# A language-model tower layer: the inner maximum turned one step later, x turned by a DMA, attend products alternating

## The reference

```
h   = layernorm(concat(emb[x], window_mean(pca[x]) @ projw + projb) @ fusw + fusb) * ln_g + ln_b
X   = layernorm(h)
Q, V= per-head RMS norm of X @ Wq.T, X @ Wv.T      (16 heads of 16)
out = Q[l] . cumsum over l of (K outer V)          (K = X by heads)
h   = h + out
xn  = layernorm(h)
a   = quantised to 8 bits by its row's maximum(xn) @ ternary(w1).T
s   = silu(depthwise conv over 3 tokens(a))        (1024 inner channels)
h   = h + quantised to 8 bits by its row's maximum(s) @ ternary(w2).T
```

## Time and profile before

| what | value |
|---|---|
| median of 3 runs (lowest, highest) | 326.43 us (324.97, 331.29) |
| the profiled execution's own time | 326.3 us |
| its span, first to last instruction | 324.6 us |
| mean granted TensorE clock | 0.782 |
| busy PE, DVE, ACT, POOL | 244.4, 244.1, 155.6, 86.4 us (75%, 75%, 48%, 27%) |

### The profile page before, as it was taken

The page is one execution under the profiler, slowest core; times in us unless marked ns, Lnnn a source line. Parts: engine busy times, 40 slices in busy tenths (PEclk is TensorE's granted clock), DMA queues, the critical chain, the costliest instruction groups (busy, mean ns, idle before and its releaser), DMA issues.

```text
span 324.6 us, 4726 instructions
## 1 busy us (share of the span) xinstructions
PE 244.4 (75%) x1538; PEld 179.5 (55%) x1538; DVE 244.1 (75%) x667; ACT 155.6 (48%) x312; POOL 86.4 (27%) x122
## 2 busy tenths in 40 slices
PE   2547597699589975997599849986899589628534
PEld 0206466568366754785477637665667467515322
DVE  0976636765997799769976998599858996886671
ACT  1054114537563765366445752595248633635811
POOL 5020013024503440235023412251233313412300
PEclk9955789669957996699559965997589857975575
DMA  7381110110011002100210012000300030001000
GB/s 186 71 290 28 49 26 0 33 42 0 1 42 32 3 0 72 37 1 0 65 43 2 1 32 73 3 0 18 90 0 2 0 96 4 1 0 34 0 32 32
DMA packets 16745, 11.71 MB, mean 36 GB/s; under 512 B 2832, under 2 KB 15953, under 8 KB 16721
## 3 DMA queue, kind: packets, MB, share of 16 engines
q1 hardware_dynamic: 15248, 10.64, 11.7%
q10 hardware_dynamic: 1472, 0.77, 1.0%
HBM read 4.07 MB, written 2.10 MB: 19 GB/s over the span
## 4 chain that ended last, share of the span: by engine, by line
PE 42%; DVE 39%; issue 6%; POOL 5%; ACT 3%; DMA 1%; SPq 1%; POOLq 0%; DVEq 0%; ACTq 0%
PE PS L614 10%; PE PH L671 9%; DVE mx L971 8%; PE PA L565 5%; PE PO L628 5%; PE PO L645 4%; DVE xq L950 3%; DVE h L983 3%; POOL h L362 3%; DVE hid L961 3%; PE PY L685 2%; DVE y L1006 2%; DVE h L829 2%; DVE amax L935 2%; DVE xn L930 2%
## 5 line engine op out<-in xcount | busy, mean ns | idle before, releaser
L479 ACT ACTIVATE hid<-PH,cb_s,cw_x 128x256 f32<-128x256 f32 x64 | 36.1, 564 | 81.8 <-PE PH L671 81.6
L671 PE MATMUL PH<-xsT,w1q 128*128 128x256 f16 x256 | 50.6, 351 | 6.2 <-DVE hid L961 5.8
L375 POOL TENSOR_TENSOR hid<-hid,tap 128x508 f32<-128x508 f32 x32 | 40.7, 1271 | 44.1 <-DVE hid L961 44.1
L905 DVE TENSOR_TENSOR ST<-PS,tri 128x512 f32<-128x512 f32 x32 | 22.1, 690 | 29.1 <-PE PO L645 20.6
L614 PE MATMUL PS<-QP,KM 128*128 128x256 f32 x128 | 42.3, 465 | 0.0
L671 PEld LDWEIGHTS PH<-xsT,w1q 128*128 128x128 f16 x256 | 29.1, 125 | 19.3 <-DVE hid L961 10.6
L961 DVE SCALAR_TENSOR_TENSOR hid<-PH,cw_x,hid 128x254 f32<-128x254 f32 x64 | 29.7, 475 | 7.9 <-ACT tap L482 7.9
L645 PEld LDWEIGHTS PO<-VD,ST 128*64 128x64 f32 x512 | 30.4, 137 | 7.3 <-issue 6.1
L645 PE MATMUL PO<-VD,ST 128*64 128x32 f32 x512 | 33.0, 222 | 0.4 <-DVE ST L905 0.4
L614 PEld LDWEIGHTS PS<-QP,KM 128*128 128x128 f32 x128 | 26.9, 232 | 10.6 <-issue 7.1
L971 DVE TENSOR_REDUCE mx<-sl 128x256 f32<-128x1024 f32 x16 | 30.7, 1916 | 2.6 <-ACT sl L489 2.6
(11 more groups left out here) (138 smaller groups left out, 454.7 us busy)
## 6 DMA issues: line engine op xcount, KB each, us to landing
QP<-QT SPq DMA_DIRECT2D x32, 64.0 KB, 2.0
VD<-Vn SPq DMA_DIRECT2D x32, 64.0 KB, 2.0
out_dram<-y SPq DMA_DIRECT2D x8, 256.0 KB, 2.1
w_s<-in_w1T_dram SPq DMA_DIRECT2D x1, 1024.0 KB, 5.2
w_s<-in_w2T_dram SPq DMA_DIRECT2D x1, 1024.0 KB, 7.6
fusw_s<-in_fusw_dram ACTq DMA_DIRECT2D x1, 512.0 KB, 4.3
feat_p<-feat SPq DMA_DIRECT2D x7, 64.0 KB, 2.0
ids_b<-in_ids_dram SPq DMA_DIRECT2D x4, 64.0 KB, 4.2
```

Of the source, the lines that this page charges most:

```text
L375: nc.gpsimd.tensor_tensor(part, part, tap[:, c % 2, :, :, 0:T - 1], ALU.add).then_inc(tap0_ok, 1)
L479: nc.scalar.activation(hid[:, j, :, :].rearrange("p u t -> p (u t)"), hidps(j), ACT.Identity, bias=cb_s[:, j:j + 1], scale=cw_x[:, j, 1:2])
L671: ins = nc.tensor.matmul(hidps(j), w1q[:, k, j * 128:(j + 1) * 128], xsT_v[:, h, :, k, :], start=(n == 0), stop=(n == 2 * KC - 1))
L905: nc.vector.tensor_tensor(ST[k][:, :].rearrange("p (n l) -> p n l", l=C), PS[k][:, :].rearrange("p (n l) -> p n l", l=C), tri[:, None, :]. ...
```

## The change

Three edits. On PE `turn_max` of a pair moves from the end of its stage-c step to the next step, behind `scores(b, 0, 0)` and directly ahead of `spread_scale`; on DVE `hid_scales` moves from the end of the step to the next, behind `mask_state` and ahead of `quantise(d, 0)`. `transpose_xs` and `take_xs` go, with the f16 identity; SP issues one transposing DMA from xs to xsT, ahead of `spread_q`, and both `hidden` and the next `xs_high` wait for its completion. In `attend` the loops over chunk b and r are exchanged, and the state product comes first.

```diff
@@ sync @@
+            def turn_xs(g):
+                wait(sp, h_ps, 8 * g)
+                wait(sp, xs_ok, 2 * g + 2)
+                sp.dma_start_transpose(xsT[:, :].rearrange("p (n t) -> p n t", t=T),
+                                       xs[:, :, :, :].rearrange("p h u d -> p (h u d)")).then_inc(xst_ok, 16)
...
                 on(gather_features, first(a))
+                on(turn_xs, b)
                 on(spread_q, a)
                 on(store, d)
@@ scalar @@
-            act.wait_ge(pool_c, 9)
-            nc.scalar.activation(ident16[:, :], ident[:, :], ACT.Copy).then_inc(ident16_ok, 1)
...
             def xs_high(g, u):
                 wait(act, xq_ok, 2 * g + u + 1)
-                wait(act, xst_ps, g)
+                wait(act, xst_ok, 16 * g)
...
-            def take_xs(g):
-                wait(act, xst_ps, g + 1)
-                wait(act, h_ps, 8 * g)
-                nc.scalar.activation(xsT[:, :], HB[1][:, :].bitcast(F16), ACT.Copy).then_inc(xst_ok, 1)
...
-                on(take_xs, b)
@@ tensor @@
-                for b in range(2):
-                    if b == 1:
-                        nc.tensor.matmul(PO[C:T, to:to + 128], QT[:, k, u, C:T], BD[:, u * KC + k, :],
-                                         start=True, stop=False, skip_group_check=True)
-                    for r in range(NG):
-                        hp = NG * k + r
+                nc.tensor.matmul(PO[C:T, to:to + 128], QT[:, k, u, C:T], BD[:, u * KC + k, :],
+                                 start=True, stop=False, skip_group_check=True)
+                for r in range(NG):
+                    hp = NG * k + r
+                    for b in range(2):
...
-            def transpose_xs(g):
-                wait(pe, xs_ok, 2 * g + 2)
-                wait(pe, conv_ok, 8 * g)
...
             def hidden(g, j):
...
                 if j == 0:
-                    wait(pe, xst_ok, g + 1)
+                    wait(pe, xst_ok, 16 * g + 16)
...
                 on(scores, b, 0, 0)
+                on(turn_max, d)
                 on(spread_scale, d)
...
                 on(down, d)
-                on(transpose_xs, b)
                 on(sum_q, a)
-                on(turn_max, c)
@@ vector @@
                 on(mask_state, b)
+                on(hid_scales, d)
                 on(quantise, d, 0)
...
                 on(inv_roots_q, a, 3)
-                on(hid_scales, c)
```

More of the change, by code:

```diff
@@ L83, in lm_tower_kernel @@
         ident = sb("ident", [128, 128])
-        ident16 = sb("ident16", [128, 128], F16)
         ones = sb("ones", [128, 128])
@@ L183, in lm_tower_kernel @@
         pf_ps, pf_ok, tab_ps, tab_ok = sem("pf_ps"), sem("pf_ok"), sem("tab_ps"), sem("tab_ok")
-        ld_pf, ident16_ok = sem("ld_pf"), sem("ident16_ok")
+        ld_pf = sem("ld_pf")
         wabs_ok, wsum_ps, w_ok = sem("wabs_ok"), sem("wsum_ps"), sem("w_ok")
@@ L204, in lm_tower_kernel @@
         a_c = sem("a_c")
-        xq_ok, xs_hi, xs_ok, xst_ps, xst_ok = (sem(n) for n in ("xq_ok", "xs_hi", "xs_ok", "xst_ps", "xst_ok"))
+        xq_ok, xs_hi, xs_ok, xst_ok = (sem(n) for n in ("xq_ok", "xs_hi", "xs_ok", "xst_ok"))
         h_ps, tap1_ok, tap0_ok, conv_ok, silu_ok = (sem(n) for n in (
```

## The result

The changed kernel takes 343.1 us (median of 4 runs, 339.38 to 345.56) against 325.7 for the kernel before: a ratio of 1.052, with an interval of 1.041 to 1.063. Slower, and within a tenth of a microsecond of the 343.0 on record. Some executions of a kernel are 1.5% to 3% longer than its fastest, most of them at a lower granted clock; the medians of this document count them, the ratios and intervals leave them out.

A forecast was written before the change was run, and what follows sets the result against it. VectorE from the third mask to finish, then TensorE, was taken to bound each step; waits +13.8 and +2.5, front -4.5, DMA +0.9 and +1.8, attend -2.4, clock +4.6 gave +16.7 on 326.3: 343.0 us, range 328 to 362.

The forecast's parts named there:

- The path and its two halves: In a 34.3 us step VectorE bounds from the third mask to finish, then turn_max and TensorE's chain.
- The wait ahead of spread_scale: TensorE's spread_scale waits for the masks and hid_scales on VectorE: +2.3 us in each of steps 3 to 8, 13.8 us.
- The turning DMA: The DMA on SP that turns xs into xsT takes 4.5 us, between bounds of 2.1 and 16.
- The terms of +1.8 and +0.9 for steps 2 and 3: Hidden products start later, waiting for the DMA's xsT: +1.8 us in step 2, +0.9 in step 3.
- Step 9: hid_scales stands behind convs 0 and 1 on VectorE, so hidden product 2 starts 2.5 us later.
- Attend: Faster products in the attend call before the third mask: 0.3 us a call, eight pairs, -2.4 us.
- The clock: TensorE's clock rises later, after the second scores, in four of six steps: +4.6 us.
- rival 1: The DMA turning x is slow, making xsT last at the front of steps 2 to 9; 371 at 8 us; chance 0.20.
- Rival 2: Stall mostly repaid: DMA takes 2.1 us, clock doesn't mind, attend gains 0.5; +5.0, 331.3 us; chance 0.18.
- Rival 3: Without the pause before turn_max, TensorE's clock rises before state: 318.0 us; chance 0.12.
- front of steps 4 to 8: With turn_max gone from between sum_q and the hidden products, state starts 0.9 us earlier: -4.5 over five steps.

The follow-up runs named there:

- filler: Changed kernel with eight more f16 products, results unused, between turn_max and spread_scale on TensorE: 331.44 us, ratio 1.015.
- move_alone: Kernel before with only turn_max and hid_scales moved into the next step; x still turned on TensorE, old attend order: 352.13 us, ratio 1.086.
- scales_first: Changed kernel with hid_scales ahead of the two masks, mask_scores and mask_state, on VectorE: 341.96 us, ratio 1.050.
- dma_alone: Kernel before with only x turned by the DMA; turn_max and hid_scales at the end of their step, old attend order: 327.2 us, ratio 1.007.

## Why the prediction was right, and where it only came out right

- **The path and its two halves**: right. Vn took turn_max's place at the front. The rows of y in the chain of waits, in step 6 before and after:

```profile
193.60 0.79 DVE y L1006 x2
```

```profile
201.03 0.78 DVE y L989 x2
```

From y's start to state's start it takes 196.90 - 193.60 = 3.3 us before and 203.34 - 201.03 = 2.3 after: a gain of 1.0, the bound named, for the 0.9 put. VectorE's half, from the third mask to y, takes 19.2 us in steps 3 to 7 of both kernels (19.3 in step 6), so nothing was lost or won there.
- **The wait ahead of spread_scale**: the mechanism and place as put, with hscale as releaser. The term of +2.3 a step was mis-sized: 3.53 - 0.85 = 2.7. hid_scales took 208.66 to 209.68, 1.0, as put; what I missed is that spread_scale behind a pause adds its full 1.22 to the path, while behind running products its 1.06 from start to end overlaps the scores and adds 0.85. Its idle time was 1.89, put at 1.6.
- **The turning DMA**: 4.5 put, 3.1 measured, which is nearer to the store of the earlier trace rows. The terms of +1.8 and +0.9 for steps 2 and 3 are wrong by all of their size: step 2's third mask came 0.3 earlier than before, and step 3's first hidden product at 93.23, not 95.0. The Trainium skill's page "Advanced Engine Details and Errata" (X-Bar Transpose) has transposing DMAs as fast as others; the trace agrees only roughly, with 3.1 us for 256 KB against the 2.1 of the store. Its page "VectorE: DVE Perf Modes" (The three transpose paths) gives 1309 ns for one block of 128x128; no run here turns one block alone, and the estimate of 10.5 us that I worked out from it, for eight in a row, does not hold for one DMA with all eight.
- **Step 9**: +2.5 put at hidden product 2. From step 8's third mask it came 313.77 - 289.96 = 23.8 after, 296.24 - 274.62 = 21.6 before: +2.2, and +1.8 at that step's y.
- **Attend**: 0.3 a call put, 0.27 measured on the path, in six steps and not eight (-1.6 for -2.4). But beside the moved maximum its weight is ten microseconds, most of it by way of the clock as the fuse rows suggest, which I had not seen.
- **The clock**: I put +4.6, as the second scores at half clock in four of six steps. From the rows after: the second scores took 1.71 in steps 5 and 7 and 1.46 in step 6 (0.86 before), step 5's fuse 3.71 instead of 1.91 and its third scores 2.00 instead of 1.06, and step 8's two scores 3.33 instead of 1.73; against that spread_scale took 0.71 and hidden products 2 and 3 0.87 in steps 4 and 5, where the clock had risen early. Net, with the smaller differences of the six steps, about +6.1, so the term was put somewhat too low. And its course was not the one I put: I let the clock only rise late. It also rose early and fell again, and the filler shows that in all 12 us could be had from it. Treating it as a small correction to a sum of waits was the weak step: `move_alone` (352, expected 338 to 344) and `scales_first` (342, expected 331 to 337) missed my expectations, both with fuse at half clock in step 4.
- **The rivals**: rival 1 is refuted by the 3.1 us and by `dma_alone`. Rival 2 needed a clock that does not mind and an attend gain of 0.5; neither came. Rival 3 is refuted as put: the pause before turn_max is gone and state still takes 2.07, at half clock. It was near a truth all the same: behind the work put into the new pause by `filler`, the clock is up.

The whole sum beside what the chains of waits of the two profiled executions give, up to y of step 9:

| term | put | measured |
|---|---|---|
| wait ahead of spread_scale, six steps | +13.8 | +16.1 |
| front of steps 4 to 8 | -4.5 | -4.5 (1.0 won in each, 0.1 lost by state and first scores) |
| steps 2 and 3, their fronts | +2.7 | -0.7 |
| attend | -2.4 | -1.6 |
| clock (with the 0.71 of spread_scale in steps 4 and 5) | +4.6 | +6.1 |
| step 9 | +2.5 | +1.8 |
| sum | +16.7 | +17.2 (17.1 in the table above) |

The terms put too low (the wait, the clock, and attend, whose gain was smaller) and those put too high (steps 2, 3 and 9) nearly cancel: 4.6 us one way and 4.1 the other. That the sum stood within 0.1 of the median is this luck.

## What to carry to other kernels

Where two engines hand a small chain back and forth, move the first link into a pause that is already there, and leave the rest where its input is long ready; putting all links just ahead of their use turns hidden work into a wait in front of everything queued behind it. Before shortening a wait on TensorE, look at how long a known product takes right behind it (fuse at 1.98 or 3.78 here): if the clock is what the wait costs, a shorter wait may gain nothing in all, and work in its place may gain more than removing part of it. Edits must be tried together and alone, since an attend order worth nothing by itself was worth 10 us beside the moved maximum.

## What the runs showed of the hardware that was not expected

- One transposing DMA of 128 x 1024 f16 from SBUF to SBUF landed 3.1 us after issue and held the issuing queue 1.27 us, against 0.65 us for each of spread_q's issues (2.60 for four).
- Products to the upper and lower 64 rows of PSUM in turn: a call of 18 took 0.97 us from its start to the waiting mask, 1.24 with the rows in two blocks, at the same clock.
- Four small f32 products behind a pause took 1.22 us from start to end at half clock; behind running products 1.06, of which 0.2 overlapped the products before, so that 0.85 was added.
- The clock rose at the start of an idle stretch (from 0.50 to 1.00 at 169.4, with TensorE idle until 171.33) and fell in gapless work (to 0.50 at 172.9); the same idle stretch in four other steps of the same execution was at 0.50 throughout.
- Eight extra f16 products in each of six pauses took 12 us off the changed kernel and 20 us off the move alone (352.1 to 332.0).
